# A Mamba layer's sequence loop: projections and vector work placed anew over the 64 scan units, softplus in four separate steps, the first convolution tap on ScalarE

## The reference

```python
hs_res = hidden_states @ w_in.T
hs, res = (hs_res[..., :d_in], hs_res[..., d_in:])
# depthwise convolution over l with 4 taps, causal
hs = jax.nn.silu(conv(hs, w_conv))
x_dbl = hs @ w_xproj.T
dt, Bm, Cm = (x_dbl[..., :R_], x_dbl[..., R_:R_ + n], x_dbl[..., R_ + n:])
delta = jax.nn.softplus(dt @ w_dt.T + b_dt)
# z[l] = exp(delta[l] * A) * z[l-1] + delta[l] * hs[l] * Bm[l];  y[l] = sum_n z[l] * Cm[l] + hs[l] * D
y = _selective_scan(hs, delta, A, Bm, Cm, D)
y = y * jax.nn.silu(res)
return y @ w_out.T
```

## Time and profile before

| | us |
|---|---|
| median of 3 runs | 4214.2 |
| profiled execution, its own time | 4210.9 |
| span of its trace | 4209.1 |
| Mamba phase, VectorE's first scan to the last | 66.7 to 2002 |
| one sequence (64 units) in the middle | 243.0 to 251.3 |
| a scan | 2.28 |

### The profile page before, as it was taken

One profiled execution on the slowest core, in us unless ns is written; L12 is line 12 of the kernel. 1 busy time (PEld: TensorE's weight loads), 2 busy tenths in 40 slices (PEclk: granted clock), 3 DMA queues, 4 the chain that ended last, 5 costly groups with the idle time before them and its releaser, 6 DMA issues. The chain is left out here.

```text
span 4209.1 us, 125390 instructions
## 1 busy us (share of the span) xinstructions
PE 3690.9 (88%) x52170; PEld 1666.0 (40%) x52170; DVE 3403.1 (81%) x3645; ACT 2605.1 (62%) x3855; POOL 1670.6 (40%) x1054
## 2 busy tenths in 40 slices
PE   6888989798898978888389999899998999989997
PEld 3545454454545445455232323323233232332422
DVE  5788888788897888887589787897878978789786
ACT  4655546465554646465149587595875958759588
POOL 4767767676776767667320100201002010020100
PEclk8999999899999989999699999999999999999999
DMA  3434334353443435334150501405014050240500
GB/s 106 118 103 120 104 93 117 101 129 103 110 115 93 118 100 130 90 95 112 63 78 2 81 22 29 74 2 81 22 31 72 2 81 22 31 72 2 82 11 11
DMA packets 145135, 308.01 MB, mean 73 GB/s; under 512 B 24456, under 2 KB 64016, under 8 KB 144336
## 3 DMA queue, kind: packets, MB, share of 16 engines
q1 hardware_dynamic: 144592, 299.94, 32.2%
HBM read 230.66 MB, written 35.13 MB: 63 GB/s over the span
## 5 line engine op out<-in xcount | busy, mean ns | idle before, releaser
L348 POOL TENSOR_TENSOR z<-z,c_rep 128x1024 f32<-128x1024 f32 x512 | 1358.7, 2664 | 608.6 <-DVE z L815 601.9
L1361 ACT ACTIVATE probs<-ps,e_scale 128x512 f32<-128x512 f32 x2048 | 1275.4, 682 | 240.9 <-PE ps L1159 215.2
L815 DVE TENSOR_TENSOR_SCAN z<-dA,ps 128x1024 f32<-128x1024 f32 x512 | 1157.0, 2277 | 325.4 <-PE ps L406 199.9
L1486 DVE TENSOR_REDUCE neg_max<-ps 128x1 f32<-128x1024 f32 x1024 | 1223.0, 1220 | 127.4 <-PE ps L1142 122.3
L671 ACT ACTIVATE dA<-rep,a_rep 128x1024 f32<-128x1024 f32 x512 | 578.4, 1145 | 606.4 <-DVE z L815 604.4
L1159 PE MATMUL ps<-q_st,k_st 50*128 50x512 f16 x2048 | 724.9, 398 | 84.9 <-ACT probs L1361 39.4
L1142 PE MATMUL ps<-k_st,q_st 48*128 48x512 f16 x2048 | 698.0, 398 | 18.1 <-issue 14.1
L406 PEld LDWEIGHTS ps<-diag,u_t 64*64 64x64 f32 x32768 | 535.3, 137 | 412.9 <-issue 412.8
L406 PE MATMUL ps<-diag,u_t 64*64 64x64 f32 x32768 | 596.7, 224 | 108.9 <-DVE z L815 83.7
L1172 PE MATMUL ps<-probs,v_h 128*32 128x256 f32 x8192 | 658.8, 396 | 0.0
L1128 POOL COPY v_h<-v_all 128x80 f32 (+1 forms) x256 | 62.0, 244 | 1412.5 <-PE ps L1172 1412.5
(11 more groups left out here) (189 smaller groups left out, 3176.5 us busy)
## 6 DMA issues: line engine op xcount, KB each, us to landing
c_rep<-c_scratch SPq DMA_DIRECT2D x512, 256.0 KB, 4.3
rep<-delta SPq DMA_DIRECT2D x128, 256.0 KB, 4.4
q_st<-qk_halves SPq DMA_DIRECT2D x192, 128.0 KB, 10.2
k_st<-qk_halves SPq DMA_DIRECT2D x192, 128.0 KB, 10.8
qk_halves<-qk_parts SPq DMA_DIRECT2D x32, 512.0 KB, 10.1
x_nat<-in_x SPq DMA_DIRECT2D x9, 1024.0 KB, 8.7
x_rows<-x_nat SPq DMA_DIRECT2D x9, 1024.0 KB, 7.3
xT<-in_xT SPq DMA_DIRECT2D x8, 1024.0 KB, 4.9
```

The source lines that it names most:

```text
L348: pool.tensor_tensor(z[:, k % ZR, :], z[:, k % ZR, :], c_rep[:, slot, :], ALU.mult).then_inc(s_zc, 1)
L815: dve.tensor_tensor_scan(z[:, k % ZR, :], dA[:, k % AR, :], pair(1 + k % 2), 0.0, ALU.mult, ALU.add).then_inc(s_z, 1)
L1361: act.activation(probs[:, kt, half * HALF:(half + 1) * HALF], ps[:, 4 + half, :], ACT.Exp, scale=e_scale[:, h:h + 1]).then_inc(s_p, 1)
L1486: dve.tensor_reduce(neg_max[:, qt:qt + 1], pair(qt % 2), AX.X, ALU.max, negate=True).then_inc(s_mx, 1)
```

## The change

Nothing is computed anew but for the shape of softplus: before, relu was added to the log and the correction subtracted afterwards; now the correction is subtracted from relu first (`relu_less_error`), which no longer needs the log, and `make_delta` adds the two. Its four VectorE steps are functions of their own and stand behind different units, and ScalarE's log is parted from the rest (`softplus_log`), as is the layer norm's log (`log_var`). Tap 0 of the convolution is taken from VectorE to ScalarE as a second reading of the PSUM banks. `s_he` so counts two for each group. Nearly all pieces stand behind another unit than before.

Where the pieces stand on the engines that the change is about, by unit k (P(x) is a half of a projection):

| piece | before | after |
|---|---|---|
| `out_proj` tiles 0..7 (TensorE) | 9..16, one each | 10; 11, 11; 13; 15; 16, 16; 17 |
| `res_proj` 0, 1, 2, 3 (TensorE) | 17,18; 28,29; 44,45; 53,54 | 18,19; 24,26; 32,35; 52,53 |
| `in_proj` 0, 1, 2, 3 | 36,37; 41,42; 47,48; 50,51 | 40,41; 44,45; 46,47; 49,50 |
| `dt_proj` 1, 2, 3, next 0 | 0, 20, 32, 61 | 0, 20, 36, 59 |
| `x_proj` | 58, 58, 59, 59 | 56, 56, 57, 58 |
| `gate` of group 3 of the sequence before, 0, 1, 2 (VectorE) | 5, 21, 37, 53 | 4, 20, 36, 51 |
| softplus 1 on VectorE | 3, 3, 4, 5 | 2, 5, 6, 6 |
| softplus 2 | 22, 22, 23, 24 | 22, 22, 24, 26 |
| softplus 3 | 34, 34, 35, 36 | 37, 38, 39, 39 |
| next softplus 0 | 63, 63, 63, 63 | 60, 61, 61, 61 |
| `make_diag` 3, next 0, 1, 2 | 6, 63, 63, 63 | 10, 59, 59, 62 |
| convolution taps 1 to 3 | 39..41, 44..46, 49,49,50, 53,53,54 | 43,44,44; 45,47,47; 50,53,54; 54,54,55 |
| tap 0 | VectorE 38, 43, 48, 52 | ScalarE, in `take_raw`, 42, 47, 49, 53 |
| `hs_silu` 0..3 (ScalarE) | 58 | 56, 56, 56, 57 |
| `res_silu` 0..3 (ScalarE) | 21, 32, 48, 58 | 21, 29, 37, 55 |
| softplus 1, 2, 3, next 0 on ScalarE, log apart | 3, 23, 35, 63 | 2 and 8, 23 and 24, 38 and 39, 62 and 63 |
| layer norm output, 2 tiles each (ScalarE) | 25, 26, 27, 28 | 28, 32, 34, 35 |
| store of x1 and load of `x_next` (SyncE), behind the C copies | 15 and 17 | 19 and 20 |

The core of the diff, cut:

```diff
@@ tensor: units @@
-                    if 9 <= k < 17:
-                        out_proj(b, k - 9)
...
+                    if k == 11:
+                        out_proj(b, 1)
+                        out_proj(b, 2)
...
-                    if k in (58, 59) and more:
-                        if k == 58:
-                            pe.wait_ge(s_sr, b * M + 4)
-                        for m in (2 * (k - 58), 2 * (k - 58) + 1):
-                            x_proj(c, m, m)
-                    if k == 61 and more:
+                    if k == 56 and more:
+                        pe.wait_ge(s_sr, b * M + 4)
+                        x_proj(c, 0, 0)
+                        x_proj(c, 1, 1)
+                    if k == 57 and more:
+                        x_proj(c, 2, 2)
+                    if k == 58 and more:
+                        x_proj(c, 3, 3)
+                    if k == 59 and more:
                         pe.wait_ge(s_xd, c + 1)
@@ scalar: take_raw @@
+                if m == M - 1:
+                    for j in range(QN):
+                        act.wait_ge(s_rep[QN + j], c * (2 * QS * 16))
                 act.activation(raw[m % 2], pair(XP), ACT.Copy).then_inc(s_he, 1)
+                act.activation(delta[:, :] if m == M - 1 else hs[:, m, :], pair(XP), ACT.Copy,
+                               scale=w_conv[:, m, PAD:PAD + 1]).then_inc(s_he, 1)
@@ vector @@
+            def relu_less_error(b, m):
 
                 at = b * M + m
+                dve.wait_ge(s_spc, at * 2 + 1)
+                dve.scalar_tensor_tensor(out=sp_e[:, :], in0=pair(XP if at else IN), scalar=0.0, in1=sp_e[:, :],
+                                         op0=ALU.max, op1=ALU.subtract).then_inc(s_spc, 1)
+
+            def make_delta(b, m):
+
+                dve.wait_ge(s_ln, b * M + (m + 1))
+                dve.wait_ge(s_spc, (b * M + m) * 2 + 2)
+                dve.tensor_tensor(delta[:, :], delta[:, :], sp_e[:, :], ALU.add).then_inc(s_dl, 1)
@@ vector: units @@
-                    if k == 63 and more:
-                        for stage in range(4):
-                            softplus(b + 1, 0, stage)
-                        for part in range(3):
-                            make_diag(b + 1, part)
+                    if k == 59 and more:
+                        make_diag(c, 0)
+                        make_diag(c, 1)
+                    if k == 60 and more:
+                        log_error(c, 0)
+                    if k == 61 and more:
+                        relu_less_error(c, 0)
+                        make_delta(c, 0)
+                        make_u(c, 0)
+                    if k == 62 and more:
+                        make_diag(c, 2)
```

More of the change, by code:

```diff
@@ new lines, in units @@
+                    if k in (46, 47) and more:
+                        in_proj(w_hs, x_next, 2, 6, k - 46, s_ih)
+                    if k == 49 and more:
+                        pe.wait_ge(s_he, RAW * (b * M + 3))
+                    if k in (49, 50) and more:
+                        in_proj(w_hs, x_next, 3, 6, k - 49, s_ih)
+                    if k == 52 and more:
+                        pe.wait_ge(s_he, RAW * (b * M + 4))
+                    if k in (52, 53):
+                        res_proj(b, 3, k - 52)
@@ L828, in units @@
+                    if k == 16:
+                        residual(b, 2)
+                        ln_sums(b, 2)
+                    if k == 17:
+                        residual(b, 3)
+                        ln_sums(b, 3)
                     if k == 18:
                         ln_stats(b)
[L830 to L836 removed]
@@ new lines, in units @@
+                    if k == 26:
+                        make_u(b, 2)
+                    if k == 36:
+                        gate(b, 1)
+                    if k == 37:
+                        log_error(b, 3)
+                    if k == 38:
+                        relu_less_error(b, 3)
+                    if k == 39:
+                        make_delta(b, 3)
+                        make_u(b, 3)
+                    if k == 43 and more:
+                        conv(c, 0, 1)
+                    if k == 44 and more:
+                        conv(c, 0, 2)
+                        conv(c, 0, 3)
@@ L846, in _ @@
             make_diag(0, 1)
-            for stage in range(4):
-                softplus(0, 0, stage)
+            log_error(0, 0)
+            relu_less_error(0, 0)
+            make_delta(0, 0)
+            make_u(0, 0)
             make_diag(0, 2)
```

262 lines of the change are left out of this document (149 added, 113 removed).

## The result

The changed kernel takes 4058.65 us (median of 4 runs, 4047.89 to 4066.41), beside 4217.38 for the kernel before in the same set (4208.68 to 4222.07). The ratio is 0.9624, with a 95% interval of 0.9595 to 0.9653: 159 us faster. 4070 was predicted, with a range of 4020 to 4150.

The account below looks back on a forecast made before the run. VectorE's and TensorE's chains bind, each stretch lasting as long as its fuller engine. Savings of 113, 16 and 15 us make 144; 4210.9 gives 4067, the median 3 above: 4070 us, range 4020 to 4150.

Parts of the forecast that it names:

- The walk: Mamba phase: a sequence followed scan to scan in seven stretches, each as long as its fuller engine; 222.5 us for 243.0.
- The seconds: A second VectorE instruction with both inputs in SBUF behind one scan costs 3.2 us, not 1.2.
- The gate: Gate in unit 4 is done before `d_times_hs` is due; the wait of `d_times_hs` at 38 goes.
- The first ten units: Units 0–9: 5.8 us to the scan of unit 2, then VectorE alone; 31.1 us for 37.55.
- ScalarE runs four units ahead, 9 us: Cover for ScalarE's four added table loads of 1.28 us, less two saved; uncovered, 2.6 us per sequence.
- Stalls of TensorE: TensorE now and then loses 1 to 5 us on its instructions; 6 us per middle sequence, making 228.5.
- The sum: Savings of 113 us in six middle sequences, 16 in the first, 15 in the last; together 144.
- Signs named beforehand: Middle sequences 224 to 232 us; VectorE idle about 20, busy 208; scans of 58 to 61 without waits above 1 us.
- Rival 1: New waits, with several pieces due within one unit, take half the gain, 10 us per sequence: 4150 us; chance 0.23.
- Rival 2: The seconds cost little where GpSimd's multiply comes later: 3995 us at the far end, 4020 likely; chance 0.10.
- Rival 3: Slower: `x_next` reaches TensorE's unit 40 late, beyond 6 us of slack: 4238 us; chance 0.05, with other slower ways.
- Rival 4: The change does nothing, since TensorE's work is the bound and only moves: 4214 us; chance 0.05.

Follow-up runs that it names:

- the repeat: The changed kernel measured again, unchanged but for an empty line: 4060.12 us, ratio 0.9624 to the kernel before.
- the version with a diagonal in unit 1: Changed kernel with no two VectorE instructions with both inputs in SBUF behind one scan, third part of the diagonals behind unit 1: 4018.33 us, ratio 0.9532.

## Why the prediction was right, step by step

- **The walk.** Predicted and measured (median of sequences 1 to 6): units 0–9 31.1 and 31.4; 10–17 31.4 and 30.9; 18–28 34.2 and 34.1; 29–39 35.6 and 36.3; 40–46 22.2 and 22.6; 47–58 42.5 and 43.4; 59–63 25.5 and 25.7. The sum is 222.5 and 224.3, and the median sequence has 224.5. The stretches that the change was to shorten, and the earlier trace rows above all, are those that it did shorten; 10–17 stays at TensorE's rate of the earlier trace rows. One reading behind a right number was off: the walk had VectorE as the fuller engine in 29–39, where TensorE is busy for 35.10 of 35.50 us and VectorE for 32.14.
- **The seconds** at 3.2: measured 3.26 (u), 3.25 to 3.39 (taps), 4.47 (diagonal), 2.31 (delta behind PSUM). The sentence that the sum would be some 75 us less without them was tried: 73. That agreement is in part luck, since the prediction gives no working for the 75, and the 73 hold more than the seconds. VectorE's busy time was put at 208 and is 211, for the most part because some *first* steps wait too, where GpSimd lags: 2.65 for the diagonals in unit 10, 1.73 and 1.43 for the first taps in 43 and 47, 1.43 in 22, 24 and 26. This price was missing from the sum.
- **The gate**: no `d_times_hs` waits for it any more (0.0 in the group above, 3.48 in the earlier trace rows). I had given it 6 us in two stretches; undone in the changed kernel it costs 8 per sequence (234.1), alone in the kernel before it brings 7.3 (240.0). Part of this is TensorE's clock, for which the walk has no term: `d_times_hs` took 3.78 behind the wait in the earlier trace rows, where the granted clock is 0.50, and takes 1.98 at 1.00. How much of the whole gain is the clock was not measured by itself.
- **The first ten units** came to the predicted length for a reason only half named. The walk had nothing for ScalarE's log, yet its place is worth up to 1.8 us: "ScalarE runs four units ahead, 9 us" does not hold in units 2 and 3, right behind the change of sequence.
- **Stalls of TensorE**, 6 us per sequence, was the term most off. The mean of 226.2 stands 1.7 above the median of 224.5, and nearly all of it is sequence 3 (233.9), which has two stalls, of 3.50 and 2.75 us. All engines in order of time, at the first:

```profile
862.67 1.97 PE L408 MATMUL ps<-diag,u_t 64*64 64x64 f32 x118
...
868.15 0.67 PE L408 MATMUL ps<-diag,u_t 64*64 64x64 f32 x10 [3.50 <-issue]
868.75 2.07 PE L415 MATMUL ps<-hs,d_diag 128*128 128x512 f32 x2
```

  118 of 128 matmuls, then 3.50 us of nothing with all inputs at hand, then the last ten. The granted clock behind it is 0.51 for the first 3.4 us:

```profile
868.10:871.50 3.40, 3.35 (x14) 1.66 (x14) 2.58 (x2) 3.36 (x4) 1.97 (x2) 0.51 0.13 24
```

  So the stretch 29–39 is 4 us longer than its median, and 47–58, with the other stall, as much. What TensorE lacks there is, by these traces, its own program. Beside the transfers of data the trace has packets of 16 KB on a queue of kind "instruction": 289 in the Mamba phase, one for every 255 of the instructions that TensorE executes there. In three traces (the changed kernel, its repeat, the kernel before) TensorE has 25 stalls above 1.2 us, in the Mamba phase, that the profile puts down to "issue". All 25 come at the same place when its instructions are counted in blocks of 256 (the 193rd or 194th). All end 1.3 to 1.6 us after such a packet has landed, one of them 1.9 after. The packet starts 2.2 to 3.0 us before the end, for the stall of 3.50 so 0.9 after it had begun: it starts late. Why late stays open, and all of this is read from the traces; no run tested it. The place is no accident either: the repeat stalls at the same two matmuls of sequence 3, for 3.62 and 1.94.

  For the kernel before I had read the distance of the mean from sequence 4 (247.3 and 243.0) as such stalls, and that reading holds: the seven stretches of middle sequences that are over 2 us longer than in sequence 4 each hold such a stall of over 1 us, and the gap for the gate at unit 38 is 3.1 to 3.2 us in each middle sequence, so it can't part them. The mistake was to carry all 4.3 us over: in the changed kernel they are 1.7.
- **The sum**: middle sequences 6 x 21.1 = 127 for 113, the first 15.7 for 16, the last 11.1 for 15, together 154 for 144. The attention phase, which has the same program, took 8.5 us more in this profile (2215.6 from 1849.0 to the end of the span, where the earlier trace rows leave 2207.1); between the kernels here it varies by as much without an order. 4210.9 - 153.6 + 8.5 + 0.6 (a later first scan) is 4066.4, the profiled execution's own time. The median is 8 below it, where I had it 3 above. So 4058.65 is near 4070 partly by luck: the sequences gave 10 us more than forecast, and the attention phase took 8.5 of them back.
- **Signs named beforehand**: middle sequences at 223.6 to 226.4, one at 233.9 (224 to 232); VectorE idle for 12 to 15 us, 22 in that one (about 20, so less than forecast, as the stalls were); the scans of 58 to 61 wait 0.64 at most; of the idle time ahead of scans 1.3 is ScalarE's and none a DMA's; the projection in unit 40 waits 0.0.
- **Rival 1** (new waits): none came but the small ones on first steps. **Rival 2**: wrong in its premise, and its 3995 needed the multiply all but gone (3985). **Rival 3**: the mechanism is real, and the slack was put at 3 for TensorE (4.5 to 10.6 measured) and 6 in all; TensorE is nearly full from 18 to 46, and what it waits there reaches the end to some four fifths (52 of 63.8 us). **Rival 4**: TensorE's busy time per sequence fell from 213 to 207 with the same matmuls, and the sequence by 21, so its work was not the bound; in the version with a diagonal in unit 1, at 95%, it all but is.

## What to carry to other kernels

Cut the period into stretches and compare the two fullest engines in each: a piece gains by moving only where its engine has room and the other is full, and work put where its engine is the fuller one costs almost its length (3 of 3.9 us). Put at most one two-input VectorE step behind the instruction that sets GpSimd off, and spend the slot in which VectorE waits for a matmul (here unit 1) on the longest of them: the two together took 4059 to 4018. Once one engine is relieved, look again before relieving it further; of 14 us taken from VectorE 3.6 arrived, and the place of one diagonal decided on 2.3 more. And compare phases, not only totals: a phase that an edit does not touch varied by 13 us here, as much as some of the effects.
